# Longer filler products among the first units of the maxima, and the first rows of maxima stored ahead of the second batch's parts

## The chip, the cores and the metric

The kernel runs on one core of a Trainium2 chip. The metric is device microseconds of one execution of the whole program; a figure for a kernel is the median over executions. The kernel before takes 736.61 us (three executions, 735.01 to 737.72).

## The reference

One transformer block on x of 2 x 1024 x 256, float32: layer norm with adaptive scale and shift, attention with 32 query heads and 8 key heads of width 8, a gated residual, a second norm, and a feed-forward of one shared expert and 16 routed ones of which each token takes 4. Cut to the part that matters here:

```python
h = _layernorm(x) * (1 + ca) + sa
q, k, v = h @ wq, h @ wk, h @ wv          # 32 heads of 8; keys and values 8 heads of 8, each for 4 query heads
att = q @ k.T / sqrt(8)                    # per batch and head, 1024 x 1024, causal mask
y = softmax(att) @ v
x = x + ga * (y @ wo)
x = x + gb * ffn(layernorm(x) * (1 + cb) + sb)
```

The softmax subtracts each row's maximum before the exponential, so a row's maximum has to be known before its exponentials.

## The kernel before, in words

The program is written out by hand for five engines that meet only at semaphores. Each engine's instructions run in the order in which they stand. Attention runs over 16 groups (2 batches x 8 key heads); a group holds 4 query heads of one batch.

**Prologue.** Four passes of 512 tokens give queries, keys and values. Queries and keys are split into a high and a low part (`k_parts`, `q_parts`), go to DRAM (`qk_parts_out(n)`, line 660: the keys' parts and the queries' parts of pass n) and come back from there as stacks, `qs`, `km` and `ks` (`load_stacks`, `late_keys`, `score_keys`). GpSimd forms differences of keys (`differences`, line 818) in `d_parts`, which lies in the last of the three buffers `probs`; `differences_out(b)` (line 670) stores them. Passes 3 and 4 belong to the second batch, which is read from group 8 on.

**Maxima.** For each group TensorE makes 10 units. A unit is one `wide(n)` (line 1197, matmul on line 1223, two banks) and one `narrow(n)` (line 1228, matmul on line 1235, one bank); VectorE reduces the two (lines 1480 and 1490 to 1499). `wide(n)` waits until unit n-1's wide reduction is through, `narrow(n)` until unit n-1's narrow one is. In front of units 10 and 12 TensorE also makes `differences(1, ...)` (line 1262), for which ScalarE keeps the excess (`exceeding`, line 988) in `over` and `over6`. After the tenth unit of a group VectorE takes the negated maximum and transposes it (`negated`, lines 1506 and 1511), GpSimd splits it into two parts (`split_rows`, lines 846 and 848), and SyncE carries it through DRAM: `rows_in(group)` (line 704) waits for the split, stores four pieces (line 710), waits for them to land, and loads two rows into `qs` (line 715).

**Scores.** Group 0's first scores (line 1287) come after 14 units (10 of group 0, 4 of group 1). They wait for `row_in` and `ks_in`. From there on each of the ten steps of a group holds scores, one unit for a later group, exponentials on ScalarE (lines 1056 and 1061), a mask on GpSimd and the product with the values on TensorE (line 1306). At step 2 of group 0 ScalarE waits for `diff_out` (line 1044), because that step's exponentials overwrite `d_parts`. At step 8 it waits for the raw weights of the first shared expert (line 1068, `load_expert` at 748) and for the stores of pass 3.

**Among the first units.** Behind units 0 to 7 stand the fourth pass's products: keys in units 0 and 1, queries (one product of 128 x 512 each, line 1118) in units 2 to 5, values (64 columns each, line 1127) in units 6 and 7. Behind units 8 to 13 stand three filler products each (line 1358): identity by identity, 128 columns, into bank 7, read by nobody.

**SyncE's order around the change.** Stacks of groups 0 to 2, `differences_out(1)`, `qk_parts_out(3)`, `rows_in(0)`, `qk_parts_out(4)`, then the loop over the groups, which begins with `load_expert` for the first shared expert and `rows_in(1)`.

Of the kernel before, what the change touches and what calls it, by code (L numbers as in the profile page):

```python
# [23 lines left out]
P = 128  # L24
# [74 lines left out]
FIRST_IDLE = 8  # L99
# [20 lines left out]
def block_kernel(nc, x_in, wq_in, wk_in, wv_in, wo_in, wr_in, we1_in, we3_in, we2_in,  # L120
# [11 lines left out]
    with whole:  # L132
        def sb(stack, name, shape, dt):
            return stack.enter_context(nc.sbuf_tensor(name, shape, dt))
# [5 lines left out]
        bank = [psum[:, i, :] for i in range(8)]  # L140

        k_bank = 7
# [8 lines left out]
        x_sb = sb(whole, "x_sb", [P, NT, D], F32)  # L151
# [17 lines left out]
        ident = sb(whole, "ident", [P, P], F32)  # L169
# [330 lines left out]
        def q_parts_out(eng, n, m):  # L500

            b, half = (n - 1) // 2, (n - 1) % 2
            toks, gs = slice(half * TT, (half + 1) * TT), slice(b * NKV, (b + 1) * NKV)
            eng.wait_ge(lo_done, QKV * (n - 1) + m + 2)
            for part in range(2):
                eng.dma_start(q_dram[m, gs, :, part, :, toks], q_parts[half][:, part, m, :].bitcast(F32)).then_inc(qk_out[n - 1], 16)
# [111 lines left out]
        def begun(group, s):  # L618
            if group == 0:
                return NPAIR + FIRST + s + min(AHEAD - FIRST, s // 3)  # L620
            return min(NPAIR * (group + 1) + AHEAD + s, NPAIR * GROUPS)

        def slots(group, s):

            return SCORE_SLOTS * group + sum(n for _, _, n in STEPS[:s + 1])
# [11 lines left out]
        with nc.Block() as block:  # L637
            @block.sync
            def _(sp):
# [20 lines left out]
                def qk_parts_out(n):  # L660

                    b, half = (n - 1) // 2, (n - 1) % 2
                    sp.wait_ge(lo_done, QKV * (n - 1) + 1)
                    for to, at, width in K_OUT[half]:
                        sp.dma_start(k_dram[b * NKV * HD:(b + 1) * NKV * HD, :, to:to + width],
                                     k_parts[:, half, :, at:at + width]).then_inc(qk_out[n - 1], 16)
                    for m in range(DC if n > 2 else 1):
                        q_parts_out(sp, n, m)

                def differences_out(b):  # L670
                    sp.wait_ge(diff_made, 5 * (b + 1))
                    sp.dma_start(k_dram[b * NKV * HD:(b + 1) * NKV * HD, :, KD:KD + TT], d_parts).then_inc(diff_out, 16)
# [10 lines left out]
                def score_keys(group):  # L683
                    for hp in range(2):
                        load_keys(sp, group, hp, ks, slice(KY, KROW), ks_in[group % NBUF])

                for group in range(NBUF):
# [10 lines left out]
                        sp.wait_ge(ky_in[0], KEY_LOADS)  # L698
                    sp.wait_ge(ones_s, group + 1)
                    score_keys(group)  # L700
                differences_out(1)
                qk_parts_out(3)

                def rows_in(group):

                    buf = group % NBUF
                    sp.wait_ge(split, 2 * group + 2)
                    rows = m_dram[group].rearrange("s x b q -> b x s q")
                    for b in range(4):
                        sp.dma_start(rows[b], neg_parts[32 * b:32 * (b + 1)].rearrange("p s x -> p s x")).then_inc(row_out, 16)  # L710
                    sp.wait_ge(row_out, 64 * (group + 1))
                    half = REP * TC // 2
                    for hp in range(2):
                        at = 64 * hp + PROD
                        sp.dma_start(qs[buf][at:at + 2].bitcast(F32).rearrange("p h t -> p (h t)"),
                                     m_dram[group, :, hp * half:(hp + 1) * half].rearrange("s x b q -> s (x b q)"))\
                          .then_inc(row_in[buf], 16)
# [10 lines left out]
                        sp.dma_start(y_dram[GROUPS - 1, rows, :], y_sb[rows, 1, :]).then_inc(y_late, 16)  # L728

                rows_in(0)  # L730
                qk_parts_out(4)
                for group in range(GROUPS):
                    if 1 <= group < GROUPS - 2:
# [32 lines left out]
                    elif group in (NKV + 3, NKV + 4):  # L766
                        n = group - NKV - 3
# [307 lines left out]
            def _(pe):  # L1075
# [121 lines left out]
                def wide(n):  # L1197

                    group = n // NPAIR
                    w, (h0, h1), tiles, chunk, _, diagonal = WIDE[n % NPAIR]  # L1200
                    segments = [(hh, i) for hh in range(h0, h1) for i in range(*tiles)]
                    buf = group % NBUF
                    if n == 0:
                        pe.wait_ge(mod_done, 2)
                    if n % NPAIR == 0:
                        pe.wait_ge(stack_in[buf], FIRST_LOADS + LOADS * (group // NBUF))
                    elif n % NPAIR == FIRST_KY:
                        pe.wait_ge(ky_in[buf], KEY_LOADS * (group // NBUF + 1))
                    if n:
                        pe.wait_ge(wide_free, n)  # L1210
                    if OUT_AT < n <= OUT_AT + 4:
                        pe.wait_ge(resid, n - OUT_AT)
                    for k, (hh, i) in enumerate(segments):
                        key = i * P if w == P else chunk * P
                        if not diagonal:
                            at = KU + key if key + w <= TT else KY + key
                        elif i % 4 == 0:
                            at = KX + (i + 3) * P
                        else:
                            at = (KX, KX, KY)[i % 4 - 1] + key  # L1220
                        for hp in range(2):
                            rows = slice(64 * hp, 64 * hp + 64)
                            last = pe.matmul(bank[wide_bank + hp][:, k * w:(k + 1) * w], qs[buf][rows, hh, i * P:(i + 1) * P],  # L1223
                                             km[buf][rows, at:at + w], start=(k == 0), stop=(k == len(segments) - 1),
                                             skip_group_check=True)
                    last.then_inc(wide_full, 1)

                def narrow(n):

                    group = n // NPAIR  # L1230
                    hp, hh, i = NARROW[n % NPAIR]
                    buf, rows = group % NBUF, slice(64 * hp, 64 * hp + 64)
                    if n:
                        pe.wait_ge(narrow_free, n)
                    pe.matmul(bank[narrow_bank][:], qs[buf][rows, hh, i * P:(i + 1) * P], km[buf][rows, KU:KU + TT],  # L1235
                              start=True, stop=True).then_inc(narrow_full, 1)
# [16 lines left out]
                def differences(group, which, first):  # L1253

                    buf = group % NBUF
                    if which == 0:
                        pe.wait_ge(ky_in[buf], KEY_LOADS * (group // NBUF + 1))
                    i, w, heads = (TC - 2, TT // 2, range(2)) if which == 1 else (TC - 1, TT, range(which // 2, which // 2 + 1))
                    for k, hh in enumerate(heads):
                        for hp in range(2):  # L1260
                            rows = slice(64 * hp, 64 * hp + 64)
                            last = pe.matmul(bank[first + hp][:, k * w:(k + 1) * w], qs[buf][rows, hh, i * P:(i + 1) * P],  # L1262
                                             km[buf][rows, KD:KD + w], start=(k == 0), stop=(k == len(heads) - 1),
                                             skip_group_check=True)
                    last.then_inc(diff_full, 1)
# [72 lines left out]
                for n in range(begun(0, 0)):  # L1338
                    if n == 1:
                        differences(0, 0, 0)  # L1340
                    elif n == 3:
                        pe.wait_ge(over_done, 1)
                        differences(0, 1, 0)
                    elif n == 7:
                        pe.wait_ge(over_done, 2)
                        differences(0, 2, 0)
                    elif n in (10, 12):
                        pe.wait_ge(stack_in[1], FIRST_LOADS)
                        pe.wait_ge(over_done, DIFFS + n // 12)
                        differences(1, n // 12, 0)  # L1350
                    wide(n)
                    batch1_behind_wide(n)
                    narrow(n)
                    if n == FIRST_IDLE:
                        pe.wait_ge(v_done, NPASS)

                    for _ in range(3 if n >= FIRST_IDLE else 0):
                        pe.matmul(bank[k_bank][:, 0:P], ident[:], ident[:], start=True, stop=True)
                pe.wait_ge(v_done, NPASS)
                for group in range(GROUPS):  # L1360
                    for s in range(NSTEP):
# [706 lines left out]
```

## Time and profile before

| what | value |
|---|---|
| median of three executions | 736.61 us |
| the profiled execution | 733.54 us |
| its span in the trace | 731.8 us |
| mean granted clock of TensorE | 0.969 |
| TensorE matmuls busy | 691.8 us, 95% of the span |
| VectorE busy | 542.7 us, 74% |
| ScalarE busy | 493.7 us, 67% |
| GpSimd busy | 272.8 us, 37% |

The span is the time from the first to the last instruction in the trace; the 1.7 us beside it lie around it. Granted clock 1.00 is full speed (2.4 GHz) and 0.50 is half (1.2 GHz). TensorE, VectorE and the others overlap, so their shares don't add up to anything. A product of float32 by float32 shows in the trace as two matmul records; one of the rounded parts (`qs` by `km`) as one.

### The profile page before, as it was taken

What the parts mean: (1) busy time and instruction counts of PE and PEld (TensorE: products, weight loads), DVE (VectorE), ACT (ScalarE), POOL (GpSimd) and SP (SyncE); (2) the same over time, 40 slices, a digit from 0 to 9 for tenths busy, and PEclk for the clock granted to TensorE, in tenths of its full rate; (3) what the DMA queues carried; (4) which work ended last, traced back from release to release, by engine and by line L of the source; (5) the groups of instructions that cost most, each with busy time, mean ns of one, the idle gap of its engine ahead of it and who ended that gap; (6) DMA issues with size and microseconds to landing.
All of it is one profiled execution on the core that took longest, in us unless ns stands there. A gap on an engine that the chain in (4) does not pass through costs nothing. (4 is left out here: it accounts for less than half of the span.)

```text
span 731.8 us, 14620 instructions
## 1 busy us (share of the span) xinstructions
PE 691.8 (95%) x4898; PEld 437.1 (60%) x4898; DVE 542.7 (74%) x1163; ACT 493.7 (67%) x739; POOL 272.8 (37%) x332
## 2 busy tenths in 40 slices
PE   8999999999999999999999889899999999999994
PEld 7556644444444444444444435478878888888783
DVE  7877788888888888888887676457596555776487
ACT  5341488999888988889888477527555666766132
POOL 5722114332323222233323112467006724560574
PEclk9987799999999999999999999999999999999997
DMA  7845613455554554544434000279346767884443
GB/s 238 224 109 152 182 26 100 139 151 167 159 150 123 158 149 150 158 107 106 116 103 106 8 20 16 88 228 327 110 144 232 266 209 211 245 244 145 138 128 109
DMA packets 78852, 108.71 MB, mean 149 GB/s; under 512 B 16216, under 2 KB 60312, under 8 KB 77692
## 3 DMA queue, kind: packets, MB, share of 16 engines
q1 hardware_dynamic: 68268, 77.16, 36.5%
q0 software_dynamic: 9280, 29.11, 12.3%
q10 hardware_dynamic: 1232, 1.51, 0.8%
q8 instruction: 42, 0.69, 0.4%
q14 instruction: 30, 0.25, 0.1%
HBM read 59.92 MB, written 47.39 MB: 147 GB/s over the span
## 5 line engine op out<-in xcount | busy, mean ns | idle before, releaser
L1061 ACT ACTIVATE probs<-psum 128x1024 f32<-128x1024 f32 x256 | 246.4, 1027 | 44.0 <-PE psum L1287 43.6
L1480 DVE TENSOR_REDUCE max_parts<-psum 128x2 f32<-128x1024 f32 (+2 forms) x160 | 196.0, 1225 | 62.2 <-PE psum L1223 60.3
L875 POOL TENSOR_SCALAR_AFFINE_SELECT probs<-probs 128x512 f32<-128x512 f32 (+1 forms) x96 | 78.8, 820 | 225.5 <-ACT probs L1061 205.3
L1306 PE MATMUL psum<-probs,v_aug 128*32 128x512 f32 (+3 forms) x1536 | 158.1, 499 | 0.3 <-POOL probs L875 0.2
L1287 PE MATMUL psum<-qs,ks 64*128 64x512 f32 (+3 forms) x768 | 135.7, 393 | 11.3 <-ACT over L988 5.0
L1287 PEld LDWEIGHTS psum<-qs,ks 64*128 64x128 f32 x768 | 65.3, 185 | 109.6 <-ACT probs L1061 68.0
L1841 PE MATMUL psum<-w_all,v_aug 128*128 x376 | 96.8, 380 | 0.9 <-ACT v_aug L1739 0.9
L1223 PE MATMUL psum<-km,qs 64*128 64x128 f32 (+2 forms) x608 | 77.7, 327 | 4.9 <-DVE max_parts L1480 3.0
L1841 PEld LDWEIGHTS psum<-w_all,v_aug 128*128 128x128 f32 x376 | 70.9, 190 | 11.2 <-issue 1.6
L1739 ACT ACTIVATE v_aug<-psum,modc 128x128 f32<-128x128 f32 x188 | 75.7, 453 | 0.2 <-PE psum L1822 0.2
L1306 PEld LDWEIGHTS psum<-probs,v_aug 128*32 128x32 f32 x1536 | 33.9, 109 | 64.5 <-issue 61.5
L1235 PE MATMUL psum<-km,qs 64*128 64x512 f32 x160 | 67.5, 422 | 0.4 <-DVE max_parts L1495 0.4
L1747 ACT ACTIVATE v_aug<-psum 128x128 f32<-128x128 f32 x94 | 26.0, 277 | 56.9 <-PE psum L1841 56.9
L1943 DVE TENSOR_TENSOR v_aug<-v_aug,psum 128x128 f32<-128x128 f32 x94 | 26.9, 286 | 49.5 <-ACT v_aug L1747 49.2
L1223 PEld LDWEIGHTS psum<-km,qs 64*128 64x128 f32 x608 | 53.1, 193 | 15.7 <-DVE max_parts L1480 7.5
L988 ACT ACTIVATE over<-psum 128x1024 f32<-128x1024 f32 x48 | 49.3, 1027 | 19.2 <-PE psum L1262 17.4
L1860 PE MATMUL psum<-w_all,v_aug 128*128 x188 | 56.4, 383 | 0.0
L1669 POOL DMA_INDIRECT h_t<-y_sorted,posi x32 | 31.6, 987 | 53.8 <-DMA y_sorted<-late 39.9
L550 POOL DMA_INDIRECT x_sorted<-probs,posi x32 | 30.7, 959 | 46.5 <-DVE posi L309 34.3
L1499 DVE CUSTOM_DVE_ANT_0 psum<-psum,over 128x512 f32<-128x512 f32 x64 | 44.2, 691 | 0.1
L1956 DVE TENSOR_TENSOR late<-psum,gate 128x256 f32<-128x256 f32 x94 | 39.5, 421 | 1.2 <-PE psum L1860 1.1
L1056 ACT ACTIVATE probs<-psum 128x1024 f32<-128x1024 f32 x32 | 32.9, 1027 | 10.5 <-PE psum L1287 10.3
(196 smaller groups left out, 1016.4 us busy)
## 6 DMA issues: line engine op xcount, KB each, us to landing
late<-x_sorted SPq DMA_DIRECT2D x94, 128.0 KB, 3.0
y_sorted<-late SPq DMA_DIRECT2D x94, 128.0 KB, 2.4
x_sorted<-g_rows POOLq DMA_DIRECT2D x6, 1536.0 KB, 7.2
qs<-q_parts SPq DMA_DIRECT2D x62, 128.0 KB
km<-k_parts SPq DMA_DIRECT2D x62, 96.0 KB
km<-k_parts SPq DMA_DIRECT2D x64, 64.0 KB
ks<-k_parts SPq DMA_DIRECT2D x64, 64.0 KB
y_sums<-g_sign SPq DMA_DIRECT2D x16, 256.0 KB, 2.7
```

The lines of the kernel that those rows point to most:

```text
L875: pool.affine_select(out=tile, in_=tile, compare_op=ALU.is_ge, fill=0.0, base=0, pattern=[[0, REP], [0, n], [1, P]], channel_multiplier=-1 ...
L988: act.activation(to, psum[:, banks, :], ACT.Relu).then_inc(over_done, 1)
L1061: act.activation(to[:, 2 * slot:2 * slot + 2, off:TT], psum[:, banks, off:TT], ACT.Exp, scale=SCALE).then_inc(p_full, 1)
L1223: last = pe.matmul(bank[wide_bank + hp][:, k * w:(k + 1) * w], qs[buf][rows, hh, i * P:(i + 1) * P], km[buf][rows, at:at + w], start=(k == ...
L1235: pe.matmul(bank[narrow_bank][:], qs[buf][rows, hh, i * P:(i + 1) * P], km[buf][rows, KU:KU + TT], start=True, stop=True).then_inc(narrow_ ...
L1287: last = pe.matmul(bank[first + hp][:, to:to + width], ks[buf][rows, c * P:(c + 1) * P], qs[buf][rows, hh, half * TT + off:(half + 1) * TT ...
L1306: last = pe.matmul(bank[sum_bank][32 * h:32 * h + 32, off:TT], v_aug[:, at:at + 32], probs[(NSTEP * group + s) % (LAG + 1)][:, h, col:col ...
L1480: dve.tensor_reduce(out=max_parts[:, :, h0:h1, slice(*tiles), slot], in_=psum[:, wide_bank:wide_bank + 2, :].rearrange("p a (s w) -> p (a ...
L1499: dve.tensor_tensor_reduce(out=bank[narrow_bank][:], in0=bank[narrow_bank][:], in1=over[:, hp, :], scale=1.0, scalar=LEAST, op0=ALU.add, o ...
L1739: last = act.activation(xt[:, k % 2, c * P:(c + 1) * P], bank[X_BANKS[k % 2]][:, c * P:(c + 1) * P], ACT.Identity, scale=modc[:, b, 1, c, ...
L1841: last = pe.matmul(bank[U_BANKS[k % 2]][:, 0:2 * H], xt[:, k % 2, c * P:(c + 1) * P], w_all[:, bass.ds(expert[k], 1), c * 2 * H:(c + 1) * ...
L1860: pe.matmul(bank[Y_BANKS[k % 2]][:, 0:D], gt[:, k % 2, :], w_all[:, bass.ds(expert[k], 1), W13:WCOLS].rearrange("p a n -> p (a n)"), start ...
```

## The change

The filler behind units 8 to 13 becomes one product of the identity by 512 columns of `x_sb` (float32, two token tiles), in place of three of 128 columns; it still goes to bank 7 and is read by nobody. `differences_out(1)` and `qk_parts_out(3)` move from ahead of `rows_in(0)` to behind it.

```diff
                     sp.wait_ge(ones_s, group + 1)
                     score_keys(group)
-                differences_out(1)
-                qk_parts_out(3)
 
                 def rows_in(group):
...
                 rows_in(0)
+                differences_out(1)
+                qk_parts_out(3)
                 qk_parts_out(4)
                 for group in range(GROUPS):
...
                     if n == FIRST_IDLE:
                         pe.wait_ge(v_done, NPASS)
 
-                    for _ in range(3 if n >= FIRST_IDLE else 0):
-                        pe.matmul(bank[k_bank][:, 0:P], ident[:], ident[:], start=True, stop=True)
+                    if n >= FIRST_IDLE:
+                        pe.matmul(bank[k_bank][:], ident[:], x_sb[:, 0:2, :].rearrange("p n d -> p (n d)"), start=True, stop=True)
```

## Rows read from the trace of the kernel before

**Rows 1.** Busy time of each engine in one stretch: PE, PEld, DVE, ACT, POOL, clock, DMA.
```profile
200.00:400.00 200.00, 196.27 (x1745) 92.21 (x1744) 167.58 (x262) 178.75 (x192) 62.21 (x84) 1.00 0.47 131
```

**Rows 2.** Stretches, PE alone: stretch, length, busy (records), granted clock, DMA share, GB/s.
```profile
48.60:48.70 0.10, 0.10 (x4) 0.84 0.43 164
...
62.20:62.30 0.10, 0.10 (x6) 0.93 1.41 246
...
66.00:82.00 16.00, 15.93 (x63) 0.50 0.65 174
...
82.70:82.80 0.10, 0.10 (x3) 0.68 0.89 195
```

**Rows 3.** Timeline of PE from 66 us: start, us, line, operation, out<-in, records.
```profile
66.80 1.65 PE L1358 MATMUL psum<-ident 128*128 128x128 f32 x6
68.37 0.79 PE L1223 MATMUL psum<-km,qs 64*128 64x512 f32 x2
68.97 0.62 PE L1235 MATMUL psum<-km,qs 64*128 64x512 f32 x1
69.52 1.65 PE L1358 MATMUL psum<-ident 128*128 128x128 f32 x6
...
83.06 0.50 PE L1287 MATMUL psum<-qs,ks 64*128 64x512 f32 x2
```

**Rows 4.** Timeline of PE from 45 us, the fourth pass among units 0 to 2.
```profile
45.75 1.97 PE L1104 MATMUL psum<-h_t,wk_sb 128*64 128x512 f32 x2
47.65 0.79 PE L1235 MATMUL psum<-km,qs 64*128 64x512 f32 x1
...
50.38 0.50 PE L1223 MATMUL psum<-km,qs 64*128 64x256 f32 x4
50.81 1.13 PE L1118 MATMUL psum<-h_t,wq_sb 128*128 128x512 f32 x2
51.88 0.50 PE L1235 MATMUL psum<-km,qs 64*128 64x512 f32 x1
```

**Rows 5.** Timeline of DVE: end of group 0's maxima, and wide reductions under load.
```profile
70.35 0.69 DVE L1499 CUSTOM_DVE_ANT_0 psum<-psum,over 128x512 f32<-128x512 f32 x1
...
71.49 0.21 DVE L1511 STREAM_TRANSPOSE neg_max_t<-neg_max 128x32 f32<-128x32 f32 x1
...
85.66 1.23 DVE L1480 TENSOR_REDUCE max_parts<-psum 128x2 f32<-128x1024 f32 x1
...
87.49 1.23 DVE L1480 TENSOR_REDUCE max_parts<-psum 128x2 f32<-128x1024 f32 x1
```

**Rows 6.** Timeline of POOL: the second half of the first split.
```profile
72.06 0.25 POOL L848 TENSOR_TENSOR neg_parts<-neg_max_t,neg_parts 128x32 fp32r<-128x32 f32 x1
```

**Rows 7.** Timeline of SP's issues: start, us of issuing, line, transfer, count.
```profile
68.02 0.56 SPq L672 DMA_DIRECT2D k_parts<-probs  x1
...
72.16 3.12 SPq L506 DMA_DIRECT2D q_parts<-w_hi  x4
75.33 2.14 SPq L710 DMA_DIRECT2D max_rows<-neg_parts  x4
78.87 0.53 SPq L715 DMA_DIRECT2D qs<-max_rows  x2
...
85.76 0.53 SPq L478 DMA_DIRECT2D wmod_sb<-in_L_ffn_ws_dram  x1
96.69 1.75 SPq L710 DMA_DIRECT2D max_rows<-neg_parts  x4
```

**Rows 8.** DMA issues of 40 to 110 us: transfer, count, KB, median us to landing.
```profile
k_parts<-probs SPq DMA_DIRECT2D x1, 256.0 KB, 3.1
...
max_rows<-neg_parts SPq DMA_DIRECT2D x8, 8.0 KB, 1.8
```

**Rows 9.** Timeline of ACT: exponentials of step 2 of group 0.
```profile
87.23 1.98 ACT L1061 ACTIVATE probs<-psum 128x1024 f32<-128x1024 f32 x2
```

## The prediction, made before the changed kernel ran

> **What bounds the kernel now.** I read the page for its shares, then the table of stretches for the attention loop, then the same table for TensorE alone around the edited units, then the timelines of TensorE, VectorE, GpSimd and SyncE from 45 to 100 us. In the attention loop TensorE is busy 196.27 of 200 us at clock 1.00 [rows 1]: it is the bound, so whatever time group 0's first scores gain or lose goes through to the end, as long as nothing else is late for them. These scores start at 83.06 [rows 3]. Before them the clock decides: it falls to half at about 62.3, stays at 0.50 through 16 us in which TensorE is busy for 15.93, and comes back at about 82.75 [rows 2]. In that stretch a whole unit (filler, wide, narrow) takes 69.52 - 66.80 = 2.72 us, of which the filler is 68.37 - 66.80 = 1.57 and wide and narrow 1.15 [rows 3]. VectorE would do with less: under load its wide reductions follow each other in 87.49 - 85.66 = 1.83 us a unit [rows 5]. So units 8 to 13 are bound by a TensorE at half clock, a good part of it on filler that nobody reads. The question is whether the new filler brings the clock back sooner.
>
> **The change, filler.** Removed: 6 times three products of 128 columns. Added: 6 times one of 512. Its shape stands in the trace at both clocks. At half clock the keys' product of unit 1 (64 weight columns, 512 moving, two records) takes 47.65 - 45.75 = 1.90 us from its start to the next instruction's; at full clock the queries' product (128 weight columns, 512 moving) takes 51.88 - 50.81 = 1.07 [rows 4]. So a filler costs 1.90 - 1.57 = 0.33 us more for as long as the clock is at half, and 0.50 less than the old one at half clock once it is full.
>
> What would the clock do? What the engine did before its rise at 48.65 [rows 2] is nearly what it will do now: a unit of the maxima and one product of 512 float32 columns at half clock, back to back [rows 4]. Afterwards it ran units with one such product each, about 1.9 to 2.3 us apart, and the clock stayed full until 62.3, where the values' products of 64 columns had taken their place. The old fillers held TensorE as busy and had no rise for 16 us. The difference is the long stream of the one product against the six short records with a weight load in front of each. I take it that the clock comes back after the first or the second new filler, at 69 to 73 us; that it comes back is well borne out by that one event, when it does is not.
>
> The Trainium skill, TensorE: Matmul & The Clock Gate, Part 1 (The HAM clock gate), says that "the default state is throttled, and activity releases the throttle", and its advice elsewhere on the page is to leave no idle gaps. By that rule alone 15.93 busy us of 16 should have released it, and the trace disagrees; a filler changed in shape and not in gaps would then bring 6 x 0.33 = 2.0 us of loss (estimate, from the rows above).
>
> The time of the units, if the clock is back at about 69.2. Filler 8 ends at 66.80 + 1.90 = 68.7, wide 9 starts 0.3 later than before. Narrow 9 follows at 69.3, filler 9 ends at about 70.7. Units 10 to 13 at full clock: wide 50.81 - 50.38 = 0.43, narrow at most 0.50 [rows 4], filler 1.07, together some 1.95 a unit (VectorE's 1.83 lies beside it), and two differences of 0.4 to 0.5 in front of units 10 and 12. 70.7 + 4 x 1.95 + 0.9 = 79.4, against 83.06: 3.7 us. If the clock is back at about 72.6, filler 9 takes 1.90 and the first difference 0.6: about 1.0 more after VectorE's own pace has taken up some of it, so 80.4, or 2.7 us.
>
> **The change, SyncE.** Scores also wait for the rows of maxima, and with the old order this would eat the gain. Before, SyncE issues the differences at 68.02 and pass 3's parts until 72.16 + 3.12 = 75.28; only then come the rows at 75.33, though the split was ready at 72.06 + 0.25 = 72.31 [rows 6, 7]. Their loads go out at 78.87 to 79.40 and land some 1.8 later by the median of the rows' stores [rows 7, 8], about 81.2; no row shows the landing of these loads themselves (from 1.3 to 3 us as the bounds, by the 1.8 and the 3.1 of the nearest transfers). So the new filler alone could gain no more than 83.06 - 81.2 = 1.9. With the new order: the maxima are ready 0.3 later (wide 9's delay through VectorE at 70.35 and 71.49 [rows 5]), so the split is ready at 72.6; from its first store to the loads' issue it took 78.87 - 75.33 = 3.54 before, and the queue is emptier now, so 3.3 to 3.5; loads out by 76.6, landed 78.4 to 79.7. That is beside TensorE's own 79.4: rows and products are ready within half a us of each other. Taken at 79.5 to 80.4 over the two clock cases, the first scores come 2.7 to 3.6 us earlier; I take 3.2.
>
> Behind `rows_in(0)` everything on SyncE shifts. It goes on at about 76.7. `differences_out(1)` (0.56 of issuing) has landed 3.1 later [rows 7, 8], at 80.4. ScalarE wants it at step 2, now at 87.23 - 3.2 = 84.0 [rows 9]: 3.6 us of cover; without it each us late is a us late for ScalarE and then for TensorE. Pass 3's parts and the differences take 75.28 - 68.02 = 7.3 of issuing, and pass 4's parts with the first expert's load 86.29 - 79.40 = 6.9 [rows 7]: SyncE is through at 76.7 + 14.2 = 90.9. Next is `rows_in(1)`, wanted at 96.69 - 3.2 = 93.5: 2.6 us of cover. The parts of the second batch are read groups later, and the expert's raw weights at step 8. All of this I cost at nothing, 0 to 1 us as the bounds, as stores of 256 KB now lie beside the first scores where before they lay beside the units.
>
> After the scores have started, units, reductions and exponentials go on as before, only sooner. The `x_sb` columns that the filler reads are written long before, and bank 7 is used by TensorE in order.
>
> **Sum.** 733.54 of the profiled execution - 3.2 = 730.3. That execution was 3.07 below the median, and the same difference on the median gives 736.61 - 3.2 = **733.4 us**. The clock's turning points need not lie at the same places in every execution, so the 20 us at half clock of this one may be shorter or longer in others; by the rows' landing at 81.2, the kernel before can't start its scores before that, so a gain of some 1.7 remains even where its clock is at its best.
>
> **The rivals.**
> *The gain is mostly given back* (735.6). The units are through at 79.4, but the rows land late, or the second batch's stores, which now run at 77 to 88 us, hold up group 0's steps or `rows_in(1)`: 1 us remains. For it: the cover of 2.6 us at `rows_in(1)` is small, and rows and products are ready together. Against: the stores' queue is empty at 72.6.
> *More than the trace shows* (731.4). The ordinary executions are 3 us longer than the profiled one; if that is a low clock that lasts into group 0's steps, the new filler takes it away too: 3.2 + 2 = 5.2 us. For it: the 3.07 us. Against: nothing in the profile shows where they are.
> *The clock isn't moved by the filler* (slower, 738.6). The six fillers then cost 6 x 0.33 = 2.0 us: scores at 85.1, and the new order gains nothing, since the products come last. 736.61 + 2.0 = 738.6. It decides if the clock comes back later than about 79: then at most one or two of the six units run at full clock and save 2.72 - 1.95 = 0.77 each, and the others lose 0.33 each. If the rise itself moved behind 83, half-clock scores add 1 to 2 us. For it: 16 busy us at half clock, and identity weights that are mostly zeros, in the old filler and the new one alike, where the queries' product had full ones. Against: the rise at 48.65. The edit of SyncE's order alone would do nothing at all in this case.
>
> **How the numbers follow.** Forecast 0.53, given back 0.19, more 0.18, clock not moved 0.10. Half a per cent (3.7 us) is about what a measurement of this kernel can tell. The forecast's own range is 732.3 to 734.5; a third of it lies below 732.9, so faster is 0.18 + 0.18 = 0.36; slower by over 740.3 is the tail of the last rival, 0.05; the rest, 0.59, is within. The range from 731.2 to 737.3 leaves out the lower part of "more" and most of the last rival.
>
> **What would show it.** In the changed kernel's trace: the granted clock back to 1.00 between 69 and 73 us, and units 11 to 13 about 1.95 apart; the filler at 1.9 us at half clock and 1.07 at full; the rows' first store right behind the split at 72.6, and their loads at about 76; the first scores (line 1287) at 79.5 to 80.4; no wait of ScalarE for `differences_out(1)`; SyncE idle again before the split for group 1. It is wrong if the clock is still 0.50 at 76, if TensorE stands in front of the first scores for over 1 us with the units done, or if the scores start over 3 us sooner and the span is not shorter by that.

## The result, and the profile after

The changed kernel takes 729.95 us (median of seven executions, 724.05 to 736.58) against 737.25 for the kernel before (seven, 735.01 to 739.3), ratio 0.9883 with a 95% interval from 0.9855 to 0.9912. The forecast was 733.4 us and 3.2 us of gain; the gain is some 7 us, and the time lies below the stated range. The profiled execution took 724.05 us, with a span of 722.3. Ratios here and below leave out executions more than 1.5% above the fastest of their kernel (one of seven here, but six of twelve in a later series on a slower chip, where the ratio flatters the edits), while medians and pooled figures take in every execution except one of 2170 us that nothing here explains. From here on "the first scores" means the start of line 1287 in group 0.

TensorE from unit 8 to the first scores, after (start, us, line, operation; compare [rows 3]):

```profile
62.09 1.12 PE L1358 MATMUL psum<-x_sb,ident 128*128 128x512 f32 x2
63.15 0.50 PE L1223 MATMUL psum<-km,qs 64*128 64x512 f32 x2
63.49 0.41 PE L1235 MATMUL psum<-km,qs 64*128 64x512 f32 x1
63.83 1.12 PE L1358 MATMUL psum<-x_sb,ident 128*128 128x512 f32 x2
...
72.57 1.12 PE L1358 MATMUL psum<-x_sb,ident 128*128 128x512 f32 x2
73.63 0.49 PE L1287 MATMUL psum<-qs,ks 64*128 64x512 f32 x2
```

The first scores come at 73.63, 9.4 us before those of [rows 3], and the filler takes 63.15 - 62.09 = 1.06 us. The clock, in the table of stretches (length, busy, clock; compare [rows 2]):

```profile
66.00:82.00 16.00, 14.13 (x76) 1.00 0.65 176
40.00:100.00 60.00, 54.90 (x345) 1.00 0.52 137
```

It never fell here between 40 and 100 us, neither among the edited units nor in the prologue at 42 us, which no edit touches. GpSimd's split and SyncE's issues (compare [rows 6, 7]; the lines moved up by two, so 708 and 713 are the rows' stores and loads):

```profile
66.54 0.25 POOL L848 TENSOR_TENSOR neg_parts<-neg_max_t,neg_parts 128x32 fp32r<-128x32 f32 x1
```

```profile
65.14 2.76 SPq L498 DMA_DIRECT2D ks<-k_parts  x4
67.94 1.85 SPq L708 DMA_DIRECT2D max_rows<-neg_parts  x4
70.84 0.54 SPq L713 DMA_DIRECT2D qs<-max_rows  x2
71.43 0.58 SPq L672 DMA_DIRECT2D k_parts<-probs  x1
...
86.22 0.48 SPq L478 DMA_DIRECT2D wmod_sb<-in_L_ffn_ws_dram  x1
87.27 1.75 SPq L708 DMA_DIRECT2D max_rows<-neg_parts  x4
```

The rows now go out right behind the third group's stacks, 7.4 us before those of [rows 7]. Behind the first scores this pair of profiles shows no difference. Before and after, in stretches of TensorE:

```profile
83.10:731.80 648.70, 613.93 (x4547) 0.99 0.48 144
```

```profile
73.60:722.30 648.70, 613.64 (x4547) 0.99 0.50 148
```

The same 648.7 us in both: all 9.5 us between these two profiles arise before the first scores, and part of them is this pair's luck with the clock: the profile of before also stood at half from 41.8 to 48.7 us, in the prologue, and that of after didn't. The medians are 7.3 apart. That the two stretches agree so well is chance too: over the 13 profiles on the faster chips, the time from the first scores to the end is 648.7 to 654.8 us, and these two have the shortest.

### The profile page after: what moved, and what is told of

Same layout as the page of the kernel before. It is cut to its first block and busy times, and to the rows that moved or that the text cites. A ratio compares the mean times of both kernels' runs of the same rounds, so it can differ in the third digit from the quotient of the medians.

```text
span 722.3 us, 14572 instructions
## 1 busy us (share of the span) xinstructions
PE 680.6 (94%) x4874; PEld 424.6 (59%) x4874; DVE 540.1 (75%) x1163; ACT 493.7 (68%) x739; POOL 272.6 (38%) x332
## 5 line engine op out<-in xcount | busy, mean ns | idle before, releaser
L875 POOL TENSOR_SCALAR_AFFINE_SELECT probs<-probs 128x512 f32<-128x512 f32 (+1 forms) x96 | 78.9, 822 | 221.1 <-ACT probs L1061 200.9
L1223 PE MATMUL psum<-km,qs 64*128 64x128 f32 (+2 forms) x608 | 74.8, 319 | 5.9 <-DVE max_parts L1480 3.1
L1306 PEld LDWEIGHTS psum<-probs,v_aug 128*32 128x32 f32 x1536 | 33.9, 109 | 64.2 <-issue 61.3
L1235 PE MATMUL psum<-km,qs 64*128 64x512 f32 x160 | 65.7, 411 | 0.7 <-DVE max_parts L1495 0.5
L1223 PEld LDWEIGHTS psum<-km,qs 64*128 64x128 f32 x608 | 50.5, 185 | 18.5 <-DVE max_parts L1480 10.6
```

The lines of the kernel that those rows point to most:

```text
L875: pool.affine_select(out=tile, in_=tile, compare_op=ALU.is_ge, fill=0.0, base=0, pattern=[[0, REP], [0, n], [1, P]], channel_multiplier=-1 ...
L1306: last = pe.matmul(bank[sum_bank][32 * h:32 * h + 32, off:TT], v_aug[:, at:at + 32], probs[(NSTEP * group + s) % (LAG + 1)][:, h, col:col ...
```

## The experiments

All kernels have one edit against the kernel before or after. Several ran in more than one series, since executions of one kernel differ by 12 us and more; "the kernel before" is always the one timed beside them on the same chip. Where a kernel ran in several series, each number names its own.

**The long filler alone** (SyncE's order as before).

```diff
-                    for _ in range(3 if n >= FIRST_IDLE else 0):
-                        pe.matmul(bank[k_bank][:, 0:P], ident[:], ident[:], start=True, stop=True)
+                    if n >= FIRST_IDLE:
+                        pe.matmul(bank[k_bank][:], ident[:], x_sb[:, 0:2, :]..., start=True, stop=True)
```

> The long filler alone; SyncE's order stays that of the kernel before. Theory A (the filler keeps the clock at 1.00 through units 8 to 13, and the rows' place in the queue then decides): the units are through by 73 to 79 us but the rows land at about 80 to 81, so the first scores stand at 80 to 81.5, TensorE waits in front of them, and the median is 1.5 to 4 us under the kernel before, that is 3 to 6 us above both edits together. Theory B (the rows were in time anyway, the filler is everything): the first scores within 1 us of both edits' and the median within 1 us of theirs. Theory C (the profiled gain is an execution's luck with the clock in the prologue): no gain over the kernel before beyond 1 us.

Measured: 736.2 us against 736.94, ratio 0.9987 (0.9963 to 1.001): nothing. The profiled execution, TensorE and who it waited for:

```profile
74.11 1.13 PE L1358 MATMUL psum<-x_sb,ident 128*128 128x512 f32 x2
81.50 0.80 PE L1287 MATMUL psum<-qs,ks 64*128 64x512 f32 x2 [6.26 <-DMA qs<-max_rows]
```

The units were through at 75.2, and TensorE stood for 6.26 us until the rows of maxima had landed. Theory A's mechanism holds, its gain of 1.5 to 4 us doesn't: the kernel before starts its scores at 81.8 to 83.1 us itself, and here the rows allowed no start before 81.5. Theory C has the number ("no gain beyond 1 us") but not the reason, since both edits together gain in every series.

**The new order alone** (short fillers; three series).

```diff
-                differences_out(1)
-                qk_parts_out(3)
...
                 rows_in(0)
+                differences_out(1)
+                qk_parts_out(3)
```

> SyncE's new order alone; the three short fillers stay. Theory A and theory B (TensorE at half clock is last in front of the first scores): rows land 3 to 7 us before they are wanted, first scores at 83 us as before, median within 1 us of the kernel before. A rival (the order brings half of the gain by itself): 3 us or more under the kernel before.

Measured: 730.92 us against 736.94, ratio 0.9927 (0.9898 to 0.9956). The rival was right and both my theories wrong: the order brings most of the gain. Its profile has a full clock from 38 to 100 us, with the short fillers:

```profile
72.25 0.94 PE L1358 MATMUL psum<-ident 128*128 128x128 f32 x6
73.49 0.50 PE L1287 MATMUL psum<-qs,ks 64*128 64x512 f32 x2 [0.30 <-DMA qs<-max_rows]
```

The first scores stand at 73.49, as early as with both edits, and TensorE waited 0.30 us for the rows. In its third series it took 731.89 against 736.11, ratio 0.9923 (0.9886 to 0.9959).

**The kernel before, once more.**

> The kernel before, once more, for the clock of each execution. Theory A (the short fillers let the clock stand at half in every execution, wherever it fell): every execution's mean granted clock is 0.965 to 0.975 and the times lie within 735 to 740. A rival (the profiled execution was an unlucky one and others go at full clock through units 8 to 13): some executions at 0.985 and under 730 us.

Measured: 736.28 us (ratio 0.9997, 0.9975 to 1.0019), twelve executions of 733.86 to 739.8, clock 0.958 to 0.977. The theory's range of clocks and times nearly holds, and its reason doesn't. The rival had the full clock through units 8 to 13 right for this profile; its times under 730 us didn't come, because a wait took their place. The profiled execution had this, in stretches of TensorE, in its timeline and in SyncE's:

```profile
48.50:78.50 30.00, 24.09 (x131) 1.00 0.66 169
79.00:85.50 6.50, 3.74 (x16) 0.50 0.67 193
```

```profile
74.26 0.94 PE L1358 MATMUL psum<-ident 128*128 128x128 f32 x6
81.76 0.80 PE L1287 MATMUL psum<-qs,ks 64*128 64x512 f32 x2 [6.57 <-DMA qs<-max_rows]
```

```profile
75.49 2.11 SPq L710 DMA_DIRECT2D max_rows<-neg_parts  x4
79.26 0.53 SPq L715 DMA_DIRECT2D qs<-max_rows  x2
```

This is what the profile ahead of the prediction could not show. With the old short fillers, the clock stayed full through units 8 to 13, the units were through at 75.2, and TensorE waited 6.57 us for rows whose split had been ready at 68.7 (68.42 + 0.25 on GpSimd) and whose stores stood behind the differences and pass 3's parts on SyncE until 75.49. During the wait TensorE did nothing and the clock fell, at 78.9, so that the first scores ran at half clock. Whether TensorE worked at half clock until 83.06 or at full clock and then waited until 81.76, the kernel before starts its scores within 1.3 us. That hides the clock. It fits that the executions of the kernel before lie closer together (733.26 to 740.61 us for 25 of them) than those of the changed kernel (724.05 to 736.58 for 7), but two profiles don't prove it for all.

**All second-batch parts ahead of the rows** (kernel before, with pass 4's parts moved too).

```diff
-                rows_in(0)
                 qk_parts_out(4)
+                rows_in(0)
```

> The kernel before with pass 4's parts also put ahead of the first rows of maxima on SyncE (4.8 us more of issuing in front of them). Theory A (in the kernel before the rows' place in SyncE's queue decides when the scores start): rows stored at 80.2 instead of 75.4, landed at 86.3, first scores there, TensorE waiting up to 11 us in front of them; median 4 to 5.5 us above the kernel before, 741 to 742.5. Rival (TensorE at half clock decides, as my prediction had it): first scores at 83 to 84.5 in the profile and the median under 739.

Measured: 741.14 us against 738.37, ratio 1.0047 (1.0023 to 1.007); 2.8 us slower.

```profile
80.82 2.02 SPq L710 DMA_DIRECT2D max_rows<-neg_parts  x4
83.90 0.53 SPq L715 DMA_DIRECT2D qs<-max_rows  x2
```

```profile
86.50 0.80 PE L1287 MATMUL psum<-qs,ks 64*128 64x512 f32 x2 [7.64 <-DMA qs<-max_rows]
```

The rows were stored 5.3 us later than in the kernel before's own second profile, the first scores came 4.7 us later than its 81.76 and 3.4 later than 83.06. The place of the wait and the landing are as theory A has them, and the rival's start at 83 to 84.5 us is ruled out. The clock had been at half from 59.5 to 76.7, so the units were through at 78.9 only, and still 7.64 us before the rows: inside this wait the half clock cost nothing. The median's 2.8 is less than the 4 to 5.5 expected. What makes up the rest isn't shown; the time behind the first scores, 648.7 to 654.8 us from profile to profile, varies by more than that.

**Both edits, five times in all** (the changed kernel and four repeats).

> Both edits, once more, for the spread over executions. Theory A: the executions differ by where the clock stands at half in the prologue (before any edited instruction) and in units 8 to 13; time follows the mean granted clock of the execution, with 724 us at 0.988 and some 731 us at 0.976. Median 728 to 732. A rival (the spread is something else, transfers say): time doesn't follow the granted clock.

> Both edits, for comparison on one chip with the order alone, without filler and with the rows still earlier. Theory A: median 727 to 730, the first scores at 73.5 to 74 us in an execution at full clock.

> Both edits, beside the fillers in units 6 and 7, the order alone and no filler on one chip. Theory A: executions of two kinds, with mean granted clock of about 0.983 to 0.988 (first scores at 73.6) and of 0.965 to 0.975 (at 82), some 8 us apart.

> Both edits, beside the version with fillers in units 6 and 7. Theory A: median 728 to 731, executions from 724 to 736.

Measured: 727.71 (ratio 0.9858, 0.9829 to 0.9887), 762.84 (0.988, 0.9843 to 0.9916), 730.62 (0.9897, 0.9863 to 0.9932) and 730.18 (0.9904, 0.9866 to 0.9942). The second was on a chip on which the kernel before took 765.11 too; the extra time there lies after 480 us. Over all twelve of its executions the median is only 2.3 us under the kernel before, so its ratio proves little. The five profiles show how far the clock spreads the first scores:

| profile | clock at half before the scores, us | first scores, us |
|---|---|---|
| changed kernel | none | 73.63 |
| first repeat | none | 73.78 |
| second (the slower chip) | 44.4 to 47.7, 61.3 to 78.3 | 82.00 |
| third | 41.5 to 51.8 | 78.30 |
| fourth | 57.9 to 68.3 | 77.10 |

Mean clock and time go together (724.05 us at 0.988, 736.58 at 0.970), as expected; but there are not two kinds of execution, the clock falls in several places. The first repeat's 727.71 lies just under the 728 to 732 expected, the fourth's 730.18 within its 728 to 731. In the third repeat a fall in the prologue alone, ahead of every edited instruction, goes with first scores 4.7 us later than at full clock. The second repeat answers what the long filler costs and does at half clock:

```profile
65.04 2.07 PE L1358 MATMUL psum<-x_sb,ident 128*128 128x512 f32 x2
67.05 0.79 PE L1223 MATMUL psum<-km,qs 64*128 64x512 f32 x2
```

```profile
61.50:78.00 16.50, 16.08 (x45) 0.50 0.40 95
```

Each takes 67.05 - 65.04 = 2.01 us, and four passed before the clock came back at about 78.3. In the fourth repeat it came back at 68.3, during the second:

```profile
63.82 2.07 PE L1358 MATMUL psum<-x_sb,ident 128*128 128x512 f32 x2
65.82 0.79 PE L1223 MATMUL psum<-km,qs 64*128 64x512 f32 x2
66.42 0.62 PE L1235 MATMUL psum<-km,qs 64*128 64x512 f32 x1
66.97 1.69 PE L1358 MATMUL psum<-x_sb,ident 128*128 128x512 f32 x2
68.60 0.50 PE L1262 MATMUL psum<-km,qs 64*128 64x512 f32 x2
```

**The order alone, again, and no filler at all** (the diff is that of the second kernel, against the changed one).

```diff
-                    if n >= FIRST_IDLE:
-                        pe.matmul(bank[k_bank][:], ident[:], x_sb[:, 0:2, :]..., start=True, stop=True)
```

> SyncE's new order with the old short fillers, once more beside both edits on one chip. Theory A (order is the gain, the longer filler adds by fewer executions at half clock in units 8 to 13): median 729 to 732, 1 to 3 us above both edits. Theory B (the longer filler does nothing): within 1 us of both edits.

> The new order with the short fillers, for the share of executions in which the clock falls among units 6 to 8. If the long filler protects the clock (theory A's weaker form): median 1 to 3 us above both edits over all executions. If it doesn't: within 1 us, and in executions at half clock 1.4 us later first scores (83.4 against 82.0, as measured).

> SyncE's new order and no filler at all behind units 8 to 13. Theory A (the order is the gain; the filler only keeps the clock): units 8 to 13 run 0 to 1 us faster where the clock is full, bound by VectorE at some 1.85 us a unit, but the clock falls to half at 66 to 73 us in most executions, since only short matmuls and waits are left; the median is 0 to 4 us above both edits. Theory B (filler of either kind is useless): median 0 to 1 us under that of the order alone.

> The new order without filler. If any filler helps to keep the clock: most executions at half clock at some point of 60 to 82 us, median 2 to 5 us above both edits. If fillers of either kind don't matter: within 1 us of the order alone or below it.

Measured: order alone, on the slower chip, 756.28 against 765.11 (0.9873, 0.9826 to 0.9919), and 0.9923 as told above; no filler 758.86 (0.9937, 0.9905 to 0.9969) on the slower chip and 731.66 (0.9926, 0.9897 to 0.9956). The order's first repeat shows the other side of the coin:

```profile
72.47 1.73 SPq L708 DMA_DIRECT2D max_rows<-neg_parts  x4
75.25 0.54 SPq L713 DMA_DIRECT2D qs<-max_rows  x2
```

```profile
62.50:86.00 23.50, 23.08 (x98) 0.50 0.49 136
```

The loads of the rows went out at 75.25 and the first scores still came only at 83.42, because TensorE spent 62.5 to 86.0 at half clock. In such an execution the order brings nothing (83.06 in [rows 3], with the old order), as the prediction said of a filler that doesn't move the clock; the mistake was to take every execution of the kernel before for such a one. Pooled over all executions on the other chips: both edits 729.3 us (24 executions), order alone 731.75 (16), no filler 731.7 (6), long filler alone 736.2 (12). Both edits are 1.5 us under the order alone in the mean, with -0.5 to 3.5 by resampling. The series disagree: side by side the mean is 4.0 us lower with both edits in the first, 0.9 lower in the third, and on the slower chip 4.7 higher. That the long filler helps at all is not settled, and neither are the expectations that turn on it. Without filler the first scores came at 72.70 in one profile, 0.9 us sooner than with it:

```profile
72.70 0.79 PE L1287 MATMUL psum<-qs,ks 64*128 64x512 f32 x2 [0.35 <-DMA qs<-max_rows]
```

Yet this profile was at half clock from 64 to 81 us. The units were through by 72.3 with units 9 to 13 at half clock, where the changed kernel needs 73.6 at full; so a good part of what half clock costs among these units is the filler itself. In the other profile without filler, with half clock in the prologue and from 62.6 to 86.6 us, the first scores came at 77.07. In time, no filler is within 1 us of the order alone, by pooled medians and means, as one of its expectations has it. Its mean is 2.3 us above both edits on the other chips (0.2 to 4.5) and 2.3 below them on the slower one (-1.5 to 6.0).

**The rows still earlier** (both edits, rows ahead of the third group's score keys; the definition of `rows_in` moves up with its first call and isn't shown).

```diff
                     sp.wait_ge(ones_s, group + 1)
+                    if group == NBUF - 1:
+                        rows_in(0)
                     score_keys(group)
...
-                rows_in(0)
                 differences_out(1)
```

> Both edits, and the first rows of maxima also stand ahead of the third group's score keys on SyncE. Theory A (the rows are level with TensorE in the changed kernel): rows stored at 66.8 instead of 67.9 and landed about 1 us earlier, the units of TensorE now last at 73.6, first scores 0 to 0.3 us earlier, median within 1 us of both edits. Rival (rows still decide): 1 us earlier, and the median as well.

Measured, on the slower chip: 759.57 us against 765.11, ratio 0.9886 (0.9825 to 0.9946), that of both edits beside it 0.988. Rows stored at 66.89 and their loads issued at 69.67, 1.2 us sooner than after; first scores at 73.67, no sooner than the 73.63 of after. So at full clock TensorE's units decide in the changed kernel, as theory A said.

**Fillers behind the values' products too** (both edits, units 6 and 7).

```diff
+                    if n in (FIRST_IDLE - 2, FIRST_IDLE - 1):
+                        pe.wait_ge(lo_done, QKV * 3 + 2)
+                        pe.matmul(bank[2][:], ident[:], x_sb[:, 0:2, :]..., start=True, stop=True)
                     if n == FIRST_IDLE:
```

> Both edits, and one long filler more behind each of units 6 and 7, where the values' products of 64 columns stand and where the clock fell in six of ten profiled executions (59.5 to 64 us). Theory A (the fall comes from these units, and it decides between first scores at 73.6 and at 82 us): the clock stays full from 48 to 75 us in the profile, the two fillers cost 0 to 1 us together as TensorE waits for VectorE there, and the executions lie closer together, median 1 to 4 us under both edits. Theory B (the fall doesn't depend on these products): executions spread as with both edits, median 0 to 1 us above.

> Both edits and the two fillers more in units 6 and 7, once more beside both edits, as only four executions stood behind the first. Theory A (they keep the clock from falling at 59 to 64 us at a price of 1.4 us): median 726 to 729, 1 to 3 us under both edits, all executions within 4 us. Theory B: within 1 us of both edits, executions up to 733 and more.

The first of these expectations miscounts: the clock had fallen between 59.5 and 64 us in five of eleven profiled executions, not in six of ten. Measured: 727.17 (0.9868, 0.9842 to 0.9894; four executions, 727.05 to 729.0) and 728.04 (0.9892, 0.9852 to 0.9932; six, 726.44 to 733.51). Both profiles have a full clock from 38 us to the first scores, which come at 75.08 and 74.86, 1.2 to 1.5 us later than the best of the changed kernel.

```profile
48.00:75.00 27.00, 25.13 (x104) 1.00 0.57 129
```

Ten executions have a median of 727.6 us against 729.3 of the changed kernel's 24: the lowest measured, but the means are 0.8 us apart with an interval of -1.1 to 2.7, so not shown to beat it. The expected spread of 4 us didn't hold in the second series.

## Why the prediction was wrong

- **SyncE's queue ahead of the rows** was costed rightly: rows landed at about 81.2 in the kernel before (81.76 measured in its other profile, TensorE waiting for them, 2.0 us after the loads' issue for 1.8 forecast), and the move takes 7.3 us of issuing out of their way. From the first store to the loads' issue it took 70.84 - 67.94 = 2.90 us afterwards, and 3.40 in the profile of the order alone, for 3.3 to 3.5 forecast.
- **The step that failed**: "units 8 to 13 are bound by a TensorE at half clock", taken as the state of every execution. The sum put the units' end at 79.4 and the split at 72.6, both after a fall of the clock at 62.3. At full clock they are at 73.6 and 66.8, and in five profiles of the changed kernel the first scores came at 73.6 to 82.0. The kernel before, with a full clock among these units, has them through at 75.2 and waits 6.6 us. So the order alone gives the gain (ratios 0.9927 and 0.9923), where the prediction let it do "nothing at all" if the filler didn't move the clock, and gave it a share of a 3.2 us gain if it did. The sentence that "a gain of some 1.7 remains even where its clock is at its best" set the best case of before (81.2) against the half-clock case of after (79.5); against 73.6 it would have read 7.6.
- **The clock back after one or two long fillers**: in one profiled fall of two, at 68.3; in the other after four, at 78.3. The one event at 48.65 [rows 2, 4] was too little to build on. With short fillers it came back after 17 to 24 us.
- **The long filler's cost**: 1.06 us at full clock (1.07 forecast), 2.01 at half (1.90 forecast, from a product with 64 weight columns).
- **Nothing given back**: right. ScalarE's step 2 ran at 77.80 without waiting for the differences, 3.6 us after the first exponential:

```profile
74.17 1.94 ACT L1061 ACTIVATE probs<-psum 128x1024 f32<-128x1024 f32 x2 [1.88 <-PE psum L1287]
...
77.80 1.97 ACT L1061 ACTIVATE probs<-psum 128x1024 f32<-128x1024 f32 x2
```

  SyncE was through with the expert's load at 86.70 and waited another 0.6 us for group 1's split before it stored those rows at 87.27, so the cover was down to 0.6 from the 2.6 forecast; after the first scores both programs take 648.7 us.
- **The rival "more than the trace shows"** came nearest (5.2 us of gain, 7.3 measured), for the wrong reason: it put the rest on half clock in group 0's steps, which the new filler would take away. The filler alone takes nothing away; the old order's wait was the rest.
- **The rival with the clock not moved** needed a clock that comes back later than about 79. In the second repeat it came back at 78.3, with the first scores at 82.0; no series made the kernel slower.

## What to carry to other kernels

When one engine seems to bound a stretch only because it runs slowly in the profiled execution, work out when each of the other paths into the same meeting point would be ready (here the rows through SyncE's queue, 81.2 us) and compare them with that engine at its full speed: two paths that end within a microsecond or two of each other hide each other. A DMA that the next phase waits for belongs ahead of stores that are read much later (here those of the second batch, read from group 8 on), and each us of issuing in front of it counts once that DMA is what the next phase waits for. Profile a kernel more than once before you call a state of the clock its own.

## What the runs showed of the hardware

The granted clock of one program differs between executions: in 17 profiled executions of the kernels here it stood at half somewhere from 41 to 52 us in eight, and fell between 57.9 and 64 us in seven. A TensorE busy for 23.08 of 23.5 us stayed at half clock. The Trainium skill, TensorE: Matmul & The Clock Gate, Part 1 (The HAM clock gate), says that activity releases the throttle, and that the turning points vary between runs with the phase of a free-running measurement. These profiles agree that the points vary; that a phase is the reason, no run shows. With the first they disagree, if activity is the busy time that the profile counts.

In all three profiles in which TensorE waited over 6 us for the rows, the clock was at half for the first scores (78.5 to 85.4 us, 78.9 to 85.8 and 83.4 to 90.3). The Trainium skill, same page (Why this matters for your kernels), warns of idle gaps between bursts of matmuls, and there the traces agree. But no such gap was needed: in the third repeat of both edits the clock fell at 82.4 with TensorE busy for 9.08 of the 10 us up to 82, and in the third series of the order alone at 82.0 with 8.98 of 10.
